# Masking the third key tile of a masked attention layer behind the exponential, on POOL, in place of a matmul ahead of it

## What is computed

```python
scores = jnp.einsum('bhqd,bhkd->bhqk', Q, K) * scale
scores = jnp.where(attn_mask[:, None, :, :], -jnp.inf, scores)
A = jax.nn.softmax(scores, axis=-1)
out = jnp.einsum('bhqk,bhkd->bhqd', A, V)
out = out.transpose(0, 2, 1, 3).reshape(Bv, Tq, Dm)
return jnp.einsum('btd,od->bto', out, Wo) + bo
```

## Time and profile before

| | us |
|---|---|
| median of 3 runs | 1936.78 (1934.66 to 1944.47) |
| the profiled execution | 1936.28, its span 1934.6 |
| PE busy | 1524.4 (79% of the span) |
| DVE busy | 851.5 (44%) |
| ACT busy | 653.0 (34%) |
| POOL busy | 455.6 (24%) |
| the masked attention | 1399 to 1666, some 267 |

### The profile page before, as it was taken

The page is one execution under the profiler, slowest core; times in us unless marked ns, Lnnn a source line. Parts: engine busy times, 40 slices in busy tenths (PEclk is TensorE's granted clock), DMA queues, the critical chain, the costliest instruction groups (busy, mean ns, idle before and its releaser), DMA issues. The chain is left out here.

```text
span 1934.6 us, 32382 instructions
## 1 busy us (share of the span) xinstructions
PE 1524.4 (79%) x11694; PEld 1145.9 (59%) x11694; DVE 851.5 (44%) x2392; ACT 653.0 (34%) x1291; POOL 455.6 (24%) x414
## 2 busy tenths in 40 slices
PE   4898984698888899999999474775489999428992
PEld 2555652366655568888888243553256666327992
DVE  4556445467766422122222453443467777430111
ACT  1443341465544302222222013442255555202320
POOL 0212110011224445666664100000011111130003
PEclk9999996699999999999999685997689999758996
DMA  5663563765552216777775254442375554218994
GB/s 239 201 189 127 170 199 93 168 135 126 115 122 63 79 41 178 209 189 204 194 197 135 72 154 115 106 104 59 120 158 132 126 131 111 68 61 320 347 334 134
DMA packets 311866, 291.37 MB, mean 151 GB/s; under 512 B 146620, under 2 KB 285204, under 8 KB 306132
## 3 DMA queue, kind: packets, MB, share of 16 engines
q1 hardware_dynamic: 267732, 258.89, 47.0%
q0 software_dynamic: 41152, 28.50, 7.6%
q10 hardware_dynamic: 2880, 2.62, 0.4%
HBM read 207.40 MB, written 82.32 MB: 150 GB/s over the span
## 5 line engine op out<-in xcount | busy, mean ns | idle before, releaser
L2056 PE MATMUL cross_ps_score<-cross_q,cross_k 128*128 128x250 f32 x1024 | 221.8, 374 | 0.8 <-DVE cross_q L2471 0.8
L2056 PEld LDWEIGHTS cross_ps_score<-cross_q,cross_k 128*128 128x128 f32 x1024 | 194.3, 190 | 23.4 <-DVE cross_q L2471 1.0
L1416 ACT ACTIVATE attn_prob<-attn_ps_prob 128x400 f32<-128x400 f32 (+2 forms) x256 | 127.1, 504 | 156.7 <-PE attn_ps_prob L1306 155.5
L2480 DVE TENSOR_TENSOR cross_prob<-cross_act_,cross_ps_score 128x250 f32<-128x250 f32 x128 | 53.3, 416 | 266.7 <-ACT cross_act_ L2176 266.7
L2559 POOL DMA_INDIRECT x_sum<-cross_ye,cross_token x64 | 128.6, 2010 | 81.4 <-ACT cross_ye L2182 69.2
L1446 DVE CUSTOM_DVE_ANT_0 attn_masked_score<-attn_ps_score,attn_mask 100x361 bf16<-100x361 f32 x256 | 123.5, 531 | 53.5 <-PE attn_ps_score L1264 46.1
L2203 DVE TENSOR_REDUCE cross_nmax<-cross_ps_score 100x2 f32<-100x722 f32 x128 | 111.8, 904 | 43.7 <-PE cross_ps_score L1823 42.7
L1073 PE MATMUL queries_bank<-queries_xt,packed_sb 128*128 128x400 f32 x192 | 98.8, 687 | 35.1 <-ACT queries_xt L1037 27.1
L2086 ACT ACTIVATE cross_prob<-cross_ps_prob 128x400 f32<-128x400 f32 (+1 forms) x192 | 94.8, 506 | 71.1 <-PE cross_ps_prob L1857 64.7
L1264 PE MATMUL attn_ps_score<-attn_k,attn_q 96*100 96x100 bf16 (+1 forms) x512 | 82.5, 276 | 44.3 <-DMA attn_k<-k_stack 40.0
L2068 PE MATMUL cross_ps_prob<-cross_val,cross_prob 128*125 128x256 f32 x512 | 115.8, 379 | 0.0
(11 more groups left out here) (326 smaller groups left out, 2822.0 us busy)
## 6 DMA issues: line engine op xcount, KB each, us to landing
experts_w<-in_w SPq DMA_DIRECT2D x40, 1024.0 KB, 6.2
k_stack<-mixer_part SPq DMA_DIRECT2D x32, 541.5 KB, 3.7
cross_k<-k_stack SPq DMA_DIRECT2D x32, 541.5 KB
attn_k<-k_stack SPq DMA_DIRECT2D x32, 541.5 KB
cross_k<-in_wg SPq DMA_DIRECT2D x32, 512.0 KB
cross_k<-in_wu SPq DMA_DIRECT2D x32, 512.0 KB
cross_val<-in_wd SPq DMA_DIRECT2D x32, 512.0 KB
k_stack<-mixer_part SPq DMA_DIRECT2D x32, 361.0 KB, 4.8
```

Of the source, the lines that this page charges most:

```text
L1416: nc.scalar.activation(prob[0:rows_, q4 % 2, t, :], ps_prob[k % 2][0:rows_, 0:GT], ACT.Exp, scale=DH ** -0.5).then_inc(a_prob[s], 1)
L2056: ins = nc.tensor.matmul(ps_pre[m][:, side, 0:CAP], w[s][:, k, m * P:(m + 1) * P], xt[s][:, k, :], start=(k == 0), stop=(k == KD - 1))
```

## The change

For the masked layer only:

- The mask matmul goes from the slots of the third key tile (k = 2, 5, 8, 11), four of twelve in a sequence, 64 in all. DVE's masked score and row maximum stay as they were.
- Those slots' exponentials are now of unmasked scores and may be anything up to infinity where a key is masked. POOL takes the minimum of the 105x400 tile and 2.0 in place (`g_capped`), waits for that, and multiplies it with a 105x100 `keep` tile, broadcast over the four heads (`g_kept`).
- `keep` is one minus the transposed mask of the last 105 keys, made by POOL (`set_keep`) from a new input `mask_t`, which SP loads for each sequence (`load_keep`).
- The weighing's third part waits for `g_kept` in place of the exponential. Everything behind it moves one slot later: weighing to slots 5, 8, 11 and 2, shift B to 3, rows to 4, turn to 6, project to 8, shift A to 10. Score units stay.
- POOL's order in a step: mask of the next sequence, group 3 of the last one, keep tile of the next one, groups 0 to 2 of this one, base of the next one.

```diff
+            LAST_AV, SHIFT_B, ROWS, TURN, OUT, SHIFT_A = 2, 3, 4, 6, 8, 10
+            av_at = {3 * g + 5: g for g in range(NQ - 1)}
...
+                def load_keep(s, n):
+                    sp.dma_start(mask8_t[s][:], prog.ins["mask_t"][bass.ds(seq(s, n), 1)].rearrange("b n t -> n (b t)")
+                                 ).then_inc(keep_in[s], 16)
...
-                    if masked:
+                    by_matmul = masked and t < LAST
+                    if by_matmul:
                         nc.tensor.matmul(out[:, 0:GT], mask[s][:, at:at + P], prog.c("tile_diag")[0:T, :],
                                          start=True, stop=False)
...
-                        pe.wait_ge(a_prob[s], n * NPU + (q4 * NKT + t + 1 - NPU))
+                        if masked and t == LAST:
+                            pe.wait_ge(g_kept[s], n * NQ + (q4 + 1 - NQ))
+                        else:
+                            pe.wait_ge(a_prob[s], n * NPU + (q4 * NKT + t + 1 - NPU))
...
+                def set_keep(s, n, before):
+                    g.wait_ge(*before)
+                    g.wait_ge(keep_in[s], n * 16)
+                    g.sem_inc(g_order, 1)
+                    nc.gpsimd.tensor_scalar(keep[s][:], mask8_t[s][:], -1.0, 1.0, ALU.mult, ALU.add).then_inc(g_keep[s], 1)
+
+                def keep_probs(s, n, q4, before):
+                    g.wait_ge(*before)
+                    g.wait_ge(a_prob[s], n * NPU + (q4 * NKT + NKT - NPU))
+                    here = prob[0:TAIL, q4 % 2, LAST, :].rearrange("p (h t) -> p h t", h=G)
+                    g.sem_inc(g_order, 1)
+                    nc.gpsimd.tensor_scalar(here, here, 2.0, None, ALU.min).then_inc(g_capped[s], 1)
+                    g.wait_ge(g_capped[s], n * NQ + (q4 + 1 - NQ))
+                    nc.gpsimd.tensor_tensor(here, here, keep[s][:].unsqueeze(1).broadcast_to([TAIL, G, T]),
+                                            ALU.mult).then_inc(g_kept[s], 1)
...
                 def step(s, n, n_prev, n_next):
                     if n_next is not None:
                         if masked:
                             set_mask(1 - s, n_next, n_prev, (g_base[s], n))
-                        set_base(1 - s, n_next, (g_mask[1 - s], n_next) if masked else (g_base[s], n))
+                            if n_prev is not None:
+                                keep_probs(1 - s, n_prev, NQ - 1, (g_mask[1 - s], n_next))
+                            set_keep(1 - s, n_next, (g_kept[1 - s], n_prev * NQ) if n_prev is not None
+                                     else (g_mask[1 - s], n_next))
...
+                        for q4 in range(NQ - 1):
...
+                            keep_probs(s, n, q4, before)
+                        if n_next is not None:
+                            set_base(1 - s, n_next, (g_kept[s], n * NQ - 1))
```

More of the change, by code:

```diff
@@ L218, in host_layout @@
         "mask": inp["mask_BxSxS2_bk1"],
+        "mask_t": inp["mask_BxSxS2_bk1"][:, :, S2 // P * P:].transpose(0, 2, 1),
         "packed": packed,
@@ L1112, in stage_attention @@
         av_at = {3 * g + 4: g for g in range(NQ - 1)}
+        if masked:
+            LAST_AV, SHIFT_B, ROWS, TURN, OUT, SHIFT_A = 2, 3, 4, 6, 8, 10
+            av_at = {3 * g + 5: g for g in range(NQ - 1)}
     else:
@@ L1121, in stage_attention @@
         half_in = [pair(f"half_in{h}_") for h in range(2)]
-        src_in, x_in, mask_in = pair("src_in"), pair("x_in"), pair("mask_in")
-        g_base, g_mask = pair("g_base"), pair("g_mask")
+        src_in, x_in, mask_in, keep_in = pair("src_in"), pair("x_in"), pair("mask_in"), pair("keep_in")
+        g_base, g_mask, g_keep, g_capped, g_kept = (
+            pair(n) for n in ("g_base", "g_mask", "g_keep", "g_capped", "g_kept"))
         pe_score, v_max = pair("pe_score"), pair("v_max")
@@ L1158, in stage_attention @@
             mask = [sbuf(f"mask{s}", [T, M_SPAN], BF16) for s in range(2)]
+            LAST = NKT - 1
+            TAIL = KEYS[LAST][1]
+            mask8_t = [sbuf(f"mask8_t{s}", [TAIL, T], U8) for s in range(2)]
+            keep = [sbuf(f"keep{s}", [TAIL, T]) for s in range(2)]
             masked_score = sbuf("masked_score", [T, HH, NK], BF16)
@@ L1224, in step @@
                         load_x(s, n + 1)
+                        if masked:
+                            load_keep(s, n + 1)
                         sp.wait_ge(pe_prob[s], n * NPU - NPU // 2)
@@ L1237, in _ @@
                         load_mask(s, 1)
+                        load_keep(s, 1)
                     load_half(s, 1, 1)
@@ L1307, in prob_unit @@
                                                k_sb[s][:, h // HH, at_k:at_k + WIDE_K],
-                                               q_sb[s][:, h // HH, at_q:at_q + T], start=not masked,
-                                               stop=not masked or j == G - 1)
+                                               q_sb[s][:, h // HH, at_q:at_q + T], start=not by_matmul,
+                                               stop=not by_matmul or j == G - 1)
                     ins.then_inc(pe_prob[s], 1)
@@ L1558, in head @@
                         set_mask(s, n, None, None)
-                    set_base(s, n, (g_mask[s], n) if masked else None)
+                        set_keep(s, n, (g_mask[s], n))
+                    set_base(s, n, (g_keep[s], n) if masked else None)
                 def step(s, n, n_prev, n_next):
```

16 lines of the change are left out of this document (15 added, 1 removed).

## The result

The changed kernel takes 1945.70 us in the median of 16 runs (1937.92 to 1957.70), the kernel before 1935.24 in 16 runs beside them (1926.30 to 1944.47). The ratio is 1.0057, 95% interval 1.0039 to 1.0074: slower by some 7.5 to 14 us, just over what can be told from no change (the forecast gave 0.47 to slower by over 0.5% and 0.45 to no change; 0.57% lies close to their border). The profiled execution took 1939.94 us (span 1938.3), at the fast end of its kernel's runs. It is only 3.66 above the profiled execution of before, because the stages that were not touched took some 7 us less in it; they vary like that from run to run (the masked stage starts between 1402 and 1421 us in the eleven traces). From the first mask tile of POOL to the end of the last `xo` of DVE it is 260.05 us before and 270.80 after, 10.75 more.

The account below looks back on a forecast made before the run. PE was taken to set the pace, busy 216 of 225 us. Fourteen periods 0.61 us longer (8.6) plus 2.4 in the last sequence made 11.0 on 1936.28, so 1947 us, range 1936 to 1958.

Parts of the forecast that it names:

- the loop: Masked stage's steady periods: fourteen, each 0.61 us longer, 8.6 us in all.
- the tail: Last sequence: the final weighing waits for POOL's minimum and product, which nothing covers, adding 2.4 us.
- the wait for POOL: Weighing of group 1: its third part waits 0.1 to 0.2 us for POOL's product.
- the held cast: DVE's split ahead of project: POOL's product holds its cast until 8.45 instead of 7.92, so project starts at 9.15.
- The mask matmul at 0.17: PE's prob slots: each mask matmul costs 0.17 us, so removing four saves 0.68 us in a sequence.
- The order, +0.6: PE stalls from later slots: plus 0.3 us at rows, 0.1 at slot 2, 0.5 at u7, minus 0.3 at u4.
- walked: PE's new period stepped through from slot 0: rows 4.36, project 9.15, u7 11.95, next slot 0 at 16.1 us.
- POOL at weighing and project, +0.65: Group 1's weighing and project: waiting for POOL's product and the held cast add some 0.65 us to a period.
- Minimum 1.24, product 0.959: POOL's two new instructions on 400 elements: 1.24 us (bounds 0.48 and 1.3) and 959 ns; a pair 2.4 us.
- The much slower rival: DVE subtractions with two SBUF inputs are held too, project starts 1.2 us later: 1964 us in all, chance 0.10.
- Small loss: Cast not held, or minimum only 0.7 us: period 15.6 to 15.7, total 1940 us, chance 0.35.
- Faster: Waits at rows, project and u7 don't grow, the 0.68 us counts in full: 1928 us, chance 0.13.

Follow-up runs that it names:

- e1: Kernel before with only the new slots, all mask matmuls kept, no new POOL work: period 16.11 us, ratio 1.0026 to the kernel before.
- e2: Kernel before with the new slots, the third key tile's mask matmul left out and nothing in its place (wrong output): period 15.42 us, ratio 0.9994.
- e3: Kernel before in its old slots, third key tile's mask matmul left out, nothing in its place (wrong output): period 14.97 us, ratio 0.9949.
- e5: Changed kernel with DVE's first split moved behind the copy of the turned rows: period 15.79 us, ratio 1.0056 to the kernel before.
- e4: Changed kernel with the split's cast written as a maximum of two equal inputs: period 15.98 us, ratio 1.0053 to the kernel before.
- e6: Changed kernel with the first split behind the turned rows' copy and score units u1, u7 a slot later: period 14.99 us, ratio 0.9968 to before.
- e7: Changed kernel with split and two score units moved, last sequence masked by matmul without POOL pairs: period 14.99 us, ratio 0.9960 to the kernel before.
- e9: Changed kernel without POOL's minimum, only its product (no cap on masked weights): period 15.42 us, one run, 1944.57 us.
- e8: Kernel before with new slots, split and two score units moved, all masks by matmul, no new POOL work: period 15.31 us, ratio 0.9985.

## Why the prediction was right

Forecast 1947, measured 1945.7; forecast for the stage +11.0, measured +10.75. The mechanism was right: the order costs more than the removed matmuls give, and POOL's pair adds to it at weighing and project. That the stage came out within 0.25 us is in part luck: the loop was 0.8 us too dear, the tail 0.6 us too cheap, and inside the loop the wait for POOL was too small and the held cast too large. The parts, one by one:

- **The mask matmul at 0.17, four in a period 0.68.** e1 less e2 gives 0.69. In the old order 0.17 of it would have gone into a wait for DVE (e3).
- **The order, +0.6** (0.3 at rows, 0.1 at slot 2, 0.5 at u7, less 0.3 at u4). e1 measured +0.62. By places, counted from slot 0 in the rows above: rows at 4.33 (walked 4.36), weighing of group 1 at 7.86 (7.91), project at 9.09 (9.15), u5 at 10.04 (10.10). Only u7 came clearly earlier, at 11.76 in place of 11.95: the stop there is 0.39 and not 0.51, behind a slot that came 0.07 earlier, and this is most of why the period is 15.99 and not 16.1.
- **POOL at weighing and project, +0.65.** e2 to the change measures 0.58. The sum was right and its parts were not. Charged were 0.1 to 0.2 for the wait and 0.45 for the held cast. Measured are 0.38 and 0.20. The unheld two thirds of weighing end at 7.86 + 0.44 = 8.30 (two thirds of 0.66), the third part came at 8.59, and from its start to project it takes 0.31 at the least (e5). So project could not have started before 8.90 in any case, 0.2 after the 8.7 that the walk had. From the end of the exponential to the product's end it takes 2.52 us (1514.80 to 1517.32) and not 2.4, and weighing's third part takes 0.31, not a third of 0.66. The held cast only adds the rest, to 9.09.
- **Minimum 1.24, product 0.959.** Measured 1.205 and 1.032. (The rows that the product was reckoned from, L1544 and L698, are additions.) The pair with its hand-overs takes 2.33 us from the minimum's start to the product's end (1514.99 to 1517.32). The lower bound of 0.48 was far off, and so was the estimate of 0.6 us from the Trainium skill (GPSIMD Engine Reference, section Performance versus the Vector engine): the minimum with one input is slower than the product with two.
- **The tail, +2.4.** Mis-sized, by 0.57. From slot 0 of the last sequence to the end it is 17.40 before and 20.37 after, +2.97, and e2 has 15.72. The last sequence has no score units between its slots, so less of PE's work covers POOL's pairs, and the third part of group 1 waits there 0.56 besides the 2.09 at the end. The forecast had only the last wait. PE's matmuls behind it ran at a lower clock, which adds 0.74 (last section). The loop's surplus was a little less than forecast: to the last slot 0 it is 7.78 us, against 8.6.
- **The much slower rival.** It was refused for a reason that holds only in part. The prediction read L1465's 169 ns maximum as a sign that two SBUF inputs are not held. In the masked stage before, those rows stand beside POOL's mask tile or in a gap: at 1461.49 the subtraction starts 0.79 into the mask tile of 1460.70 and takes 0.17. Beside POOL's product an instruction with two SBUF inputs is held (e4). In the changed kernel's loop the subtraction never meets the product, since it starts right behind the held cast: 1517.38 is after the product's 1517.32 and ahead of the next minimum at 1517.69. The rival needed it held through that minimum, and beside a minimum e6 and e7 have it 28 times, 0.57 to 0.84 into it, always at 0.17. No trace has it within the first 0.5 us of a minimum, so there it stays open. The rule of the Trainium skill (GPSIMD Engine Reference, section Key points) names both kinds of DVE instruction: beside POOL's product the trace agrees for both, beside its mask tile and its minimum it does not for two SBUF inputs.
- **Small loss** asked for a cast that is not held, or a minimum of 0.7. e5 has the cast out of project's way and 15.79, above the rival's 15.6 to 15.7, because the wait at weighing stays. e9 has no minimum at all and 15.42, below them. **Faster** asked that rows, project and u7 find their partners ready; e6 comes near that case, but only once the units are moved.

The signs named ahead came as they were named: period, minimum, idle ahead of rows (0.83), ahead of project on the turned copy (0.35 on the weight load) and ahead of u7 (0.22). One did not: the cast's median stayed at 172 ns. Neither sign of being wrong came: the period is over 15.5, and PE's wait for POOL's product, 2.2 us in all and 5.1 on the weight loads, is less than that at rows (10.8 and 12.8).

The tail's rows, PE and POOL in the last sequence after:

```profile
1660.60 0.38 PE L1340 MATMUL attn_ps_acc<-attn_prob,attn_val 105*32 105x100 f32 x8 [0.56 <-POOL attn_prob L1589]
...
1664.05 1.21 POOL L1587 TENSOR_SCALAR attn_prob<-attn_prob 105x400 f32<-105x400 f32 x1 [0.97 <-ACT attn_prob L1436]
1665.34 1.03 POOL L1589 TENSOR_TENSOR attn_prob<-attn_prob,attn_keep 105x400 f32<-105x400 f32 x1
...
1666.42 0.38 PE L1340 MATMUL attn_ps_acc<-attn_prob,attn_val 105*32 105x100 f32 x8 [2.09 <-POOL attn_prob L1589]
...
1667.50 1.07 PE L1349 MATMUL attn_ps_misc<-packed_sb,attn_acc 128*100 128x128 f32 x4 [0.70 <-ACT attn_acc L1447]
...
1670.43 2.03 PE L1363 MATMUL attn_ps_misc<-packed_sb,attn_turned 128*100 128x256 f32 x4 [0.46 <-DVE attn_turned L1507]
```

## What to carry to other kernels

Work that goes from the busiest engine to an idle one must be handed over in time: compare the time of the whole new chain (two instructions and all hand-overs, 2.58 us from the exponential's end at 1514.80 to the waiting matmul at 1517.38) with the distance that the order leaves (2.29, to 1517.09, where the rest of weighing is through), and if the order is moved to make that distance, move the filler work of every slot with it. Price the order and the work apart, by one kernel with the new order alone. In the last pass, where little covers the chain, the work can stay on the old engine (e7).

## What was not expected of the hardware

- **The clock at the end.** Windows of three us, the last ones of the stage, first after and then e2 (columns as in the earlier trace rows, the clock is the number behind POOL's):

```profile
1664.02:1667.02 3.00, 0.68 (x24) 0.24 (x12) 0.00 (x0) 0.15 (x1) 2.23 (x2) 0.94 0.02 6
...
1670.02:1673.02 3.00, 2.03 (x4) 0.99 (x4) 0.78 (x2) 0.00 (x0) 0.00 (x0) 0.50 0.00 0
```

```profile
1667.80:1670.80 3.00, 1.50 (x6) 0.79 (x6) 1.20 (x3) 0.00 (x0) 0.00 (x0) 1.00 0.00 0
```

  The granted clock fell to 0.50, the 1.2 GHz level, behind PE's 2.09 us wait for POOL's last product, and stayed at 1.00 in e2, where PE had no such wait. Project at the end takes 2.03 us in the first and 1.11 in the second, rows 1.07 and 0.62. The kernel before stands between: rows 0.61, project 1.95. So against the kernel before the low clock adds 0.46 us at rows, 0.20 at the turn (0.59 against 0.39) and 0.08 at project to the wait itself. A wait for POOL is not needed for the clock to fall: in e7 and e8, where PE has none in the last sequence, rows takes 0.61 and project 2.03, while in e1 and e3 project takes 1.11. What decides between those is open.
- **Whether POOL holds a DVE instruction depends on POOL's instruction too.** Beside POOL's fp32 product, which has two tensor inputs, the small splits of DVE are held to its end: with one SBUF input (0.80 us, 0.17 alone) or two (0.79), they end within 0.04 us of it, and so does every split beside POOL's fp32 addition for the base (0.57 for the maximum of e4, started 0.09 into it). DVE instructions that read PSUM, such as the row maxima, kept their 0.53 to 0.54 beside the product. Beside POOL's instructions with one tensor input, the mask tile and the minimum, splits with two SBUF inputs that started 0.43 us or more into them took 0.17 in all cases: 88 subtractions in nine traces and 14 maxima in e4. The cast beside the mask tile took 0.17 where it started 0.42 to 0.60 into it, and was held to its end where it started 0.67 to 0.85 into it, as in the earlier trace rows. The few splits that started in the first 0.3 us of a mask tile or a minimum were held until 0.50 to 0.55 into it and no longer (the cast at 1426.34 beside the mask tile of 1426.19: 0.36). Why is open; no run was made for it.
- **A minimum costs POOL more than a product.** 1205 ns for 105x400 with one fp32 tensor and a constant, 1032 ns with two tensors, one of them broadcast over the heads.
